# A new order of the same instructions on every engine of a two-layer decoder kernel

## Chip, cores and metric

The kernel runs on one core of one Trainium2 chip. A core has TensorE (PE in the profile, with its weight loads as PEld), VectorE (DVE), ScalarE (ACT), GpSimd (POOL) and SyncE (SP, which here only issues DMAs). The metric is the device time of one execution in microseconds (us), the median of the runs. Everything is in 32-bit floats.

## What is computed

Eight sequences of 256 rows by 256 columns go through six blocks, each added to its input and followed by a layer norm:

```python
x = _layernorm(x + _L0_attn_ref(...))   # selective scan: in-projection, convolution of 4 taps, 16 states, gate, out-projection
x = _layernorm(x + _L0_xattn_ref(...))  # cross term with the context, 192 columns
x = _layernorm(x + _L0_ffn_ref(...))    # feed-forward, 1024 hidden, low-rank experts, best two of four
x = _layernorm(x + _L1_attn_ref(...))   # attention, 16 query heads, 4 key heads, rotary
x = _layernorm(x + _L1_xattn_ref(...))  # cross attention to the context
x = _layernorm(x + _L1_ffn_ref(...))    # recurrent gates, carried from sequence to sequence
```

The state of the last block runs through the eight sequences in order, and all outputs need the final state. So the program ends with a short stage for all eight sequences at once.

## The kernel before

One sequence is a batch b, from 0 to 7. The work on it is cut into streams, one letter each. F is the front of the scan block (norm, projections, convolution, softplus, gates). S is the scan itself: 16 steps of [128 x 1024] for each batch. G is the gate, out-projection and norm behind the scan. W holds the cross term and the feed-forward of batch b (the x functions), between them the last two blocks of batch b-1 (the z functions), and at the end the final stage (the e functions). Y is the attention's projections and scores, V its values and out-projection. Every stream is a Python generator on each engine; a piece between two `yield`s is a unit.

Nothing sorts the work at run time. Each engine takes its instructions strictly in program order. That order is written out by hand or by a planner in the table `ORDER`: a string of letters for each engine, and `play` lets the stream named by each letter go on by one unit. Inside a stream the order is fixed. Between the engines semaphores hold everything in place, so that any order without a deadlock computes the same.

The streams overlap. While DVE scans batch b, PE works on the attention of b-1, on the feed-forward of b-1 and on the front of b+1. One scan step on DVE is three instructions in SBUF alone: the product for the next step (line 567), the scan (576), the product with C (584). From the third batch on, a DMA that GpSimd issues (609) adds halves of the result before PE turns and sums it (512).

The norms tie GpSimd to DVE. `stats_end` takes mean and variance on DVE; its last instruction (267) writes the variance. GpSimd then runs `rstd`: a power (275) and a product (276), both of [128 x 2]. ScalarE applies them (`normal`, 279), and PE turns the result (`turn`, 286). Each batch has seven such places: a (front), a1 (behind the scan), b1 and f1 (W, first half), c2 and c1 (W, second half) and t (V). An eighth one, rn, has two powers (881) behind DVE's 805. Over eight batches that makes 64 places. The t place has one more power behind it (1375).

Lines that the prediction speaks of, beside these: 1311 and 1312 are the rotary products (one input in PSUM), 1336 is the maximum of the scores (input in PSUM), 1349 the weighing of values, 1342 a reciprocal of [128 x 4], 1103 and 1104 the update of the recurrent state (two inputs in SBUF), 1201, 1210, 1229 and 1234 the matmuls of scores, turns, row sums and values.

```python
def rstd(pool, own, tag):
    own.link(pool.tensor_tensor(ln_rs[tag][:, :], ln_var[tag][:, :], neghalf[:, 0:T], ALU.pow))
    return pool.tensor_tensor(ln_nb[tag][:, :], ln_nm[tag][:, :], ln_rs[tag][:, :], ALU.mult)
```

Of the kernel before, what the change touches and what calls it, by code (L numbers as in the profile page):

```python
# [44 lines left out]

ORDER = {
    "pe": (
        "FFFFFFFFFSSWFSFFSWSYSWSYFSFSFSFYSWSSSSSSFYGGGFGSSYYWWWYYWYWYSFYSWYWYWSYWWWFYWYFSSWWWWFWSWWSWWWWWSSYYYYYYYSYYSY"
        "SYYYYYSWSYYVSYFYVYGGGYYGYVSSYWWYWVYWYFSWYFYVYWSWFWYVYWWWSYWYWVWYWWFWYYSVWWSVWWSWWWVFVVSYSWWYYWYWYSWFYWYYYSYWSY"
        "WWYWWYSWWSYWWYSYVYSFYGYVYGWGGYYSSYWWVWYSYVWYWYFYFYWVWYWSYSVWYWYWSWYVWYWFWYWSYVWVSWWVWWWWWSVVFSYWFYWYYWSYWYYWYY"  # L50
        "WYSWYSWWYWWSYWYWWYSYSWYVFSYYGGYVWFYGYVYGFYYSSYWWWYSFWVWYSFYSWWWVYYFWYWWYVYWWSYWVWWYYWVSWWVWWWWWSVSVVWFSYWYYSWY"
# [9 lines left out]
        "YSWYWSSYWSYYSSWWSWFSSWYYSYWYYSYSVWYYYGYSSWVGYYYYSFGSSWYYVWYYSVSFYYFYYWWYVYFWYSYSSWVWYYWSYYWSVSYWYFWYYSVSWFSWFS"
        "WSWWSFYWFVWSWSYWSWYYSWYWSSYWSWSYSYSWYWYYYWSSWSYYVYYFSGSYYFVGSYYWVFYYYYGSSWYFWFSYYSVYFFSSWSWFYYWYVYWWYYWSYYWVSS"
        "YWYVWYYWVSWFWSSSWWSSWYFSWVWWYSWWSWSYYYSSWSWYYSWYWSSYYWYYSWSYVSYYYFSSWSYGGVYYYYGYVSWSYYWFYYSYYVFSFYWYSWFSYVWYFW"
        "FWFSWYYWYYFSVWWYYVSSWYYWWFSSVSSSWWWSYVWWWSWSYSYWSWYSSWYSYWYSWYWFSSYYWYYSWSYVYSYSYSFWVSGYYGYYYYGVSWYYFWSVYYFYYS"
        "FWVWYYSYWYSFSWFYVYWWYYSSVFWYYWYYWVWWSSWSSSWWFSYSSVWSYYSWWWSYWFSSWYWYYYSWWSYYSYWYWSSYYWVSFSSYYSWGVYYGSYYSWFYVGY"
# [5 lines left out]
        "FWFFFFFSWSFSSSFSFSSSSSFSSSSSSWSYFFSFSSSSSSSSFSFYSWSSFSWSSSSWSSSSWSSSSSSSFSSYGGSSGSSGSSYSSYYFWYYSYWYSFYYWSSWWFY"
        "SSYSFSSSWSSWSYFSSSWWYSSSSSWWSSSSYYSSSYSSSYSSYSSYYSSSYFSYYSGVYGSSYYSSVGYSYGYFSFYVSSYYWSSVYWYFSVYSWYSWWSYVYFWSYF"
        "SWFSYSVWYSYSSWSVSSSWSSWWSVVSSSYSYSSWSFSWYSYSWSSYSSSSWSSYYSSWYSFYVYGGYSSSYYSVGGSSYYYSFYVSFSWSVYYWYSSYSYWVSWYWFY"
        "YSYWVSSSYWYSWSVYFSVSFWSSSSWFSWWSVVSSYSYFSSSSYWSYWSWSSYSSSSSWYYSYSSWYYSYVGGSFSYYSYVFFGSYYVSGYSSYSSSYWFSWFFVYYYF"
        "WSWWSYSYVYWSYSVYWSYSSVYSWSWVSSSSSWWWVSSSVSYSSFYSWSSYWSWYSSSSYWSSSYSYSSYWYYSVSGGYYYSSSYVSGGYYSSYVFSSSFWYYFWYYSY"
        "SVSFWYVWWFYYFFSWSWYSSVYYWSYVSSWSSSSSFSVWWWSSVVSSSYSSYSWSSWYSWSYSSYSSSWSYYSSYWSYYFSVYSSGGYVYSSGYGYYSFFSYVSYYSWV"
        "SYWYSYVFWSWYWSYYFVFYWSWYYSVSYSSWVSSFWSSVSSSSWWWSSVSYSYSSSSYSSSYWFSWYSWSSYYSSSSWYYYSSWSSFSVSYGGYYSSSYGVGYYSSVSY"
        "SSYYWSVYWSYYSVWYSWWSYYSVYWSSWYYSSYWVSSSWVSFSWSSWWVSSSVSSYSSYSWSWYSWSYSSYSWSSYYSSSSYYYWGGYYVYYGGYYVYVWYYWVYYYWV"
        "YWWVYYYWYYYWVWWVWVWWVYYYYYYYYWYYVWWYYYVYYYVYYWYVYYYWVYWYVYYYVYYVVVWWWWWWWWWWWW"
# [1697 lines left out]
```

## Time and profile before

| | us |
|---|---|
| median of 3 runs | 1268.45 |
| lowest, highest | 1267.79, 1273.7 |
| the profiled execution, its own time | 1271.64 |
| its span in the profile | 1268.9 |
| PE busy in the span | 1103.8 (87%) |
| DVE busy | 1025.4 (81%) |
| ACT busy | 762.8 (60%) |
| POOL busy | 219.6 (17%) |

The profile is one execution. Its span lies 2.74 us below its own device time, and that time lies 3.2 us above the median. In a timeline row the first number is the start from the span's begin, the second the duration, both in us. A bracket behind a row tells how long the engine sat idle before it and who released it. Ends of neighbouring instructions on DVE overlap by some 0.08 us in the records, and matmuls overlap more, so sums of single durations exceed the busy time.

### The profile page before, as it was taken

The numbers are of one execution on the slowest core, as the hardware profiler recorded it, in microseconds if no ns is written. First come the engines' busy times: TensorE is split into PE (matmuls) and PEld (weight loads), VectorE is DVE, ScalarE is ACT, GpSimd is POOL, SyncE is SP. The second block draws the span as 40 slices with busy tenths as digits, with TensorE's granted clock in tenths as the row PEclk, the third lists the DMA queues.
The fourth block names the chain that finished last, engine by engine and source line by source line (L and its number), as shares of the span: only waits on it lengthen the run. The fifth ranks groups of instructions, "written<-read, shape, count | busy, mean of one in ns | idle before, by whom it ended". The sixth has DMA issues, their size and how long they took to land.

```text
span 1268.9 us, 17417 instructions
## 1 busy us (share of the span) xinstructions
PE 1103.8 (87%) x6154; PEld 805.9 (64%) x6154; DVE 1025.4 (81%) x1690; ACT 762.8 (60%) x2010; POOL 219.6 (17%) x257
## 2 busy tenths in 40 slices
...
DMA packets 41193, 86.70 MB, mean 68 GB/s; under 512 B 3737, under 2 KB 14970, under 8 KB 40466
## 3 DMA queue, kind: packets, MB, share of 16 engines
...
q8 instruction: 48, 0.79, 0.3%
...
## 4 chain that ended last, share of the span: by engine, by line
PE 45%; DVE 28%; ACT 12%; issue 6%; POOL 5%; DMA 4%; ACTq 0%; DVEq 0%; SPq 0%; POOLq 0%
PE bank L292 14%; DVE scans L576 7%; DVE scans L584 4%; PE bank L1201 4%; PE bank L927 3%; DMA scans<-scans 3%; PE bank L1234 3%; PE bank L921 3%; PE bank L512 3%; PE bank L1210 3%; DVE conv L431 2%; ACT scans L541 2%; PE bank L692 2%; DVE scans L567 2%; PE bank L1143 2%
## 5 line engine op out<-in xcount | busy, mean ns | idle before, releaser
L541 ACT ACTIVATE scans<-dt,a_neg 128x255 f32<-128x255 f32 x512 | 225.2, 500 | 0.1
L609 POOL DMA_DIRECT2D scans<-scans x96 | 84.6, 881 | 512.6 <-DVE scans L584 512.4
L576 DVE TENSOR_TENSOR_SCAN scans<-scans 128x1024 f32<-128x1024 f32 x64 | 146.2, 2285 | 13.5 <-ACT scans L541 12.8
L584 DVE TENSOR_TENSOR scans<-scans,BC 128x1024 f32<-128x1024 f32 x128 | 155.9, 1218 | 0.1
L576 DVE TENSOR_TENSOR_SCAN scans<-scans,dBx_odd 128x1024 f32<-128x1024 f32 x64 | 146.2, 2285 | 9.2 <-ACT scans L541 9.2
L512 PE MATMUL bank<-ident,scans 128*128 128x128 f32 x640 | 105.3, 303 | 45.0 <-DVE scans L584 29.4
L1282 ACT ACTIVATE ya<-bank,nmax 128x256 f32<-128x256 f32 x256 | 117.9, 474 | 41.8 <-issue 23.5
L512 PEld LDWEIGHTS bank<-ident,scans 128*128 128x128 f32 x640 | 83.8, 156 | 70.0 <-DVE scans L584 35.2
L1336 DVE TENSOR_REDUCE nmax<-bank 128x2 f32<-128x512 f32 x128 | 83.6, 683 | 38.4 <-PE bank L1201 38.1
L1289 ACT ACTIVATE ya<-bank 128x512 f32<-128x512 f32 x128 | 73.3, 602 | 27.5 <-PE bank L1210 26.7
L1210 PE MATMUL bank<-ident,ya 128*128 128x128 f32 x512 | 76.1, 280 | 8.4 <-ACT ya L1282 8.4
L538 ACT ACTIVATE scans<-neghalf 128x4 f32<-128x4 f32 x128 | 26.6, 208 | 88.4 <-PE bank L512 88.3
L567 DVE TENSOR_TENSOR scans<-conv,BC 128x1024 f32<-128x1024 f32 x64 | 77.5, 1211 | 0.1
L567 DVE TENSOR_TENSOR dBx_odd<-conv,BC 128x1024 f32<-128x1024 f32 x64 | 77.4, 1209 | 0.0
L1201 PE MATMUL bank<-kT,qT 64*128 64x256 f32 x512 | 72.6, 402 | 5.1 <-ACT ya L1289 4.2
L1210 PEld LDWEIGHTS bank<-ident,ya 128*128 128x128 f32 x512 | 59.6, 143 | 27.4 <-ACT ya L1282 17.5
L1234 PE MATMUL bank<-ya,v 128*64 128x256 f32 x512 | 67.7, 386 | 2.4 <-ACT ya L1289 1.7
L692 PE MATMUL bank<-w_i,xT 128*128 128x512 f32 x128 | 67.2, 651 | 1.4 <-ACT wa L783 1.4
L292 PE MATMUL bank<-w_q,yT 128*128 128x512 f32 x128 | 61.6, 604 | 0.0
L1201 PEld LDWEIGHTS bank<-kT,qT 64*128 64x128 f32 x512 | 44.1, 186 | 27.3 <-issue 16.9
L1245 PE MATMUL bank<-w_ao,qT 128*128 128x256 f32 x256 | 60.3, 386 | 0.0
L737 PE MATMUL bank<-w_o,wa 128*128 128x256 f32 x256 | 57.4, 380 | 0.0
...
## 6 DMA issues: line engine op xcount, KB each, us to landing
...
```

Source lines behind the costliest of these rows:

```text
L292: last = pe.matmul(o, l, r, start=(start and i == 0), stop=(i == n - 1), skip_group_check=True)
L512: last = pe.matmul(sums_of(c, t), step_of(b, u)[:, i, t * P:(t + 1) * P], ident[:, :], is_transpose=True, start=False, stop=(h == UH - 1 a ...
L541: ins = act.activation(step[:, j, 1:S], dt[b % 2][:, c, 1:S], ACT.Exp, scale=a_neg[:, c, n:n + 1])
L567: dve.tensor_tensor(dBx[u % 2], conv[b % 2][:, c:c + 1, :].to_broadcast([P, HN, S]), Bh, ALU.mult).then_inc(s["a_dBx"], 1)
L576: dve.tensor_tensor_scan(H, H, flat(dBx[u % 2]), 0.0, ALU.mult, ALU.add).then_inc(s["a_scan"], 1)
L584: dve.tensor_tensor(H, H, Ch, ALU.mult).then_inc(s["a_hC"], 1)
L609: pool.dma_start(flat(H[:, 0:2, :]), flat(H[:, 2:4, :]), accum_op=ALU.add).then_inc(SUM_OF[(NU * b + u) % 3], 16)
L692: pe.matmul(WB[j % 2][:, :], xT[:, k, t * P:(t + 1) * P], w_i[:, k, half * 512:(half + 1) * 512], start=(k == 0), stop=False, skip_group_c ...
L1201: last = pe.matmul(YB[i][:, t * S:(t + 1) * S], qT[half, p, t * P:(t + 1) * P], k[half], start=True, stop=True, tile_position=(half.start, 0))
L1210: last = pe.transpose(YB[h % 2][:, k * S + t * P:k * S + (t + 1) * P], pe_[:, h % 2, t, k * P:(k + 1) * P], ident[:, :])
L1234: last = pe.matmul(y2[i * HD:(i + 1) * HD, 0:S], v1[:, k, g, :], pT[:, i, k, :], start=(k == 0), stop=(k == 1), tile_position=(0, i * HD))
L1282: act.activation(pe_[:, h % 2, t, :], YB[h % 2][:, t * S:(t + 1) * S], ACT.Exp, bias=nmax[:, h % 4, t:t + 1], accum_out=ls[:, p % 2, t, h ...
```

## The change

No instruction, tile, wait or DMA is added or removed; each stream keeps its own order. Only the strings in `ORDER` are new, for all five engines, with the same count of each letter. Counted out against the units, GpSimd's and SyncE's orders move by at most 6 places. On PE the units before the last G unit are 825 before and 820 after: one score unit, two turns, one value unit and one turn of W now stand behind it. On DVE they are 864 and 860.

What stands on DVE directly behind the instruction that releases GpSimd (line 267 or 805), by place and batch:

| place, batch | before | after |
|---|---|---|
| a, 1 | 584, 576 | 1470, 584 |
| rn, 1 | 584, 576 | 431, 431 |
| c2, 0 | 576, 1356 | 452, 1356 |
| c1, 0, 1 and 4 | 584, 576 | 1311, 1312 |
| a1, 2 | 584, 576 | 1336, 1336 |
| b1, 2 | 1342, 584 | 1349, 1342 |
| c2, 2 | 1356, 259, 576 | 1356, 259, 264 |
| a, 7 | 584, 1342 | 1336, 805 |
| c1, 5 | 567, 1311 | 1311, 1312 |
| a, 5 | 597, 259, 567 | 576, 1336 |
| rn, 4 | 1336, 1336 | 576, 1336 |
| a1, 6 | 1336, 1336 | 584, 1103 |

Over all 64 places the next instruction is one with both inputs in SBUF (443, 447, 567, 576, 584, 814, 1103, 1104) or a large copy-like one (1080) 21 times before and 8 times after.

```diff
     "pe": (
...
-        "WWSVSVVWYSWYYWYWYSWYYWYSWYYWWYSWYYSWYWWYYWSYWVYYSSYGGWGGVYYYWWWYVYWYWVYYYVWYWYWVWYWWYYWWYVWYYWWVWVWWVWWWWWVVYW"
-        "YYYYYYYYYWYWYYWYWYYVWYWYYWYWVWYYWYVWYYWYVWYYWYVYYVYWYYVYWYYVVVVVWWWWWWWWWWWWWWWWWWWWW"
+        "WSWVVVYVSWVWYSYYWYYWSYWYYWYWYYWYSWYWWWWWYYSSSYGWGGGYVYWYWWWVYYWYWVYYYVWYYWYVWYYWVYWYWYWWYVWYYWWVWVWWVWWWWWVVYW"
+        "YYYYYYYYWYYWYYWYWYYVWYWYYWYWVWYYWYVWYYWYVWYYWYVYYYVYWYVYWYYVVVVVWWWWWWWWWWWWWWWWWWWWW"
...
     "pool": (
-        "FFFGWWWSGFSWSWSSSSSSWWVSSSWSSSSSGSFWSWSSSSSSWWSVSSWSSSSSFSGSWSWSSSSWSWSVSSWSSSSSGSWSFWSSSSSWWSVSSSWSSSSSGFSWSW"
-        "SSSSSWWSVSSSWSSSSSGSSWWSSSSSSWWVSSSWSSSSGWWWWVWWVWWWWWW"
+        "FFGWWFWFSGWSWSSSSSSSSWWVSSSSWSSSGSFWWSSSSSSWWSVSSSSWSSSSSGSFWSWSSSSSSWWVSSSSWSSSGSSSFWWSSSSSSWWVSSSWSSSSGSSFWS"
+        "WSSSSSSWWSVSSWSSSSGSSWSWSSSSSSWWSVSSSWSSGWWWWVWWVWWWWWW"
     ),
     "sp": (
-        "WFFSWSSWFWFSGWSSFSSSWFGSSWFFSWGWSSWSFSFWWWGWSSSFWSWWGSWFSSFSFWWWGWSSSFWSWGWWSSSGWWWWWWWWW"
+        "WFSFWSSWFWWSGSSWFFSSGFSSSFSGWWWFWSSSFSGWWWFSWSSFSGWWFWSSWFSSWFGWWWSSFSSWGWWSSSWWGWWWWWWWWW"
     ),
```

## Rows read from the trace of the kernel before

**Rows 1.** The page, part 1: busy time, share of the span, instructions; and part 4, engines.
```profile
PE 1103.8 (87%) x6154; PEld 805.9 (64%) x6154; DVE 1025.4 (81%) x1690; ACT 762.8 (60%) x2010; POOL 219.6 (17%) x257
...
PE 45%; DVE 28%; ACT 12%; issue 6%; POOL 5%; DMA 4%; ACTq 0%; DVEq 0%; SPq 0%; POOLq 0%
```

**Rows 2.** Busy time by stretch: the stretch, its length, each engine's busy time, granted clock, DMA.
```profile
0.00:200.00 200.00, 136.59 (x545) 91.51 (x546) 170.21 (x224) 94.97 (x220) 14.17 (x22) 0.79 0.28 99
200.00:1070.00 870.00, 795.38 (x4613) 590.63 (x4612) 776.88 (x1229) 571.67 (x1535) 187.13 (x198) 0.96 0.30 69
1070.00:1200.00 130.00, 123.61 (x785) 88.11 (x784) 52.52 (x153) 72.03 (x206) 8.21 (x17) 1.00 0.10 35
1200.00:1269.00 69.00, 48.22 (x217) 35.69 (x215) 25.76 (x86) 24.17 (x53) 10.14 (x20) 0.92 0.09 31
```

**Rows 3.** GpSimd's four small lines: duration ns min/median/max, then each line's busy total.
```profile
L275 POOL TENSOR_TENSOR rstd_c<-var_c,neghalf x16: 688/1593/2785, 323.3 to 1229.7; 128x2 f32<-128x2 f32 x16
L276 POOL TENSOR_TENSOR shift_c<-minus_c,rstd_c x16: 194/196/2115, 326.0 to 1230.5; 128x2 f32<-128x2 f32 x16
L881 POOL TENSOR_TENSOR rn<-ss,neghalf x16: 679/699/2135, 150.6 to 1083.0; 128x2 f32<-128x2 f32 x16
L1375 POOL TENSOR_TENSOR rstd_c<-var_c,neghalf x8: 683/689/1717, 329.1 to 1213.6; 128x2 f32<-128x2 f32 x8
...
sum 1269.00, POOL 63.28; mean POOL 63.28
...
sum 1269.00, POOL 40.39; mean POOL 40.39
...
sum 1269.00, POOL 15.62; mean POOL 15.62
...
sum 1269.00, POOL 8.48; mean POOL 8.48
```

**Rows 4.** Timeline of DVE and GpSimd at place c1 of batch 1.
```profile
495.32 1.22 DVE L584 TENSOR_TENSOR scans<-scans,BC 128x1024 f32<-128x1024 f32 x1
496.46 2.29 DVE L576 TENSOR_TENSOR_SCAN scans<-scans,dBx_odd 128x1024 f32<-128x1024 f32 x1
...
495.50 1.61 POOL L275 TENSOR_TENSOR rstd_c<-var_c,neghalf 128x2 f32<-128x2 f32 x1 [9.54 <-DVE var_c L267]
497.19 1.54 POOL L276 TENSOR_TENSOR shift_c<-minus_c,rstd_c 128x2 f32<-128x2 f32 x1
```

**Rows 5.** Timeline of DVE and GpSimd at place a of batch 3.
```profile
264.55 2.28 DVE L576 TENSOR_TENSOR_SCAN scans<-scans 128x1024 f32<-128x1024 f32 x1
...
264.32 0.69 POOL L275 TENSOR_TENSOR rstd_a<-var_a,neghalf 128x2 f32<-128x2 f32 x1 [2.54 <-DVE var_a L267]
265.09 1.73 POOL L276 TENSOR_TENSOR shift_a<-minus_a,rstd_a 128x2 f32<-128x2 f32 x1
```

**Rows 6.** Timeline of DVE and GpSimd at place c1 of batch 2.
```profile
636.58 0.69 DVE L1311 TENSOR_TENSOR ya<-bank,rope 128x512 f32<-128x512 f32 x1
...
636.76 0.71 POOL L275 TENSOR_TENSOR rstd_c<-var_c,neghalf 128x2 f32<-128x2 f32 x1 [4.70 <-DVE var_c L267]
637.55 0.19 POOL L276 TENSOR_TENSOR shift_c<-minus_c,rstd_c 128x2 f32<-128x2 f32 x1
```

**Rows 7.** Chain of waits, POOL's first and last lengthened places: start, length, what.
```profile
42.88 1.61 POOL rstd_a L275
...
44.56 1.57 POOL shift_a L276
...
1039.90 1.62 POOL rstd_c L275
```

**Rows 8.** Waits, 200 to 1070 us, DVE and PE: total us, times, longest.
```profile
DVE scans L576 <- ACT scans L541: 19.8, 12, 4.8
...
PE bank L286 <- ACT x L279: 10.3, 7, 1.9
PE bank L286 <- ACT xb L279: 6.7, 3, 3.2
```

**Rows 9.** What line 1311 waited for in the whole span: us, times.
```profile
  PE bank L292: 25.0, 11
```

**Rows 10.** Chain of waits behind 1160 us, PE's attention units.
```profile
1162.93 1.06 PE bank L1201 x8
1163.99 0.58 PE bank L286 x4
1164.58 0.59 PE bank L1229 x8
1165.16 0.86 PE bank L1234 x8
...
1167.95 0.87 PE bank L1210 x8
```

More of the change, by code:

```diff
@@ L47 @@
     "pe": (
[L48 to L51, printed above, removed]
@@ L52 @@
-        "WYWSYWYWYYSWYYWYWWSYWYWWYSYWYVSFYYSYWGVGYGYGYVSSYYWWWFYWVWSYYYFSFWYYVWWFYSWVWWFWWYYWYWWVSWFYYWWVWWSWWSVWSVVVWF"
-        "YWYSWYWSYWYYSYWYWYSWYWYYWWYWYSWSWYYWYVSYFYSWVYGGGYYGYVSSYWYWWYVWFYSWYYFVWWYSWYFYWVWYWYWSVYWWYWYWVWSVWWVWSWWWSW"
-        "VFVYSFWYYYSYWYYWYSWYWYSFYWSYWYWYWWWSYYWYWWYSVSYWFSYGVGGYYGWYVSSWYYWWVSYWYWYVYWSYWWYSVYWWWYYWSWYWVWWYYSWVWWVWWW"
-        "WWSVSVVWYSWYYWYWYSWYYWYSWYYWWYSWYYSWYWWYYWSYWVYYSSYGGWGGVYYYWWWYVYWYWVYYYVWYWYWVWYWWYYWWYVWYYWWVWVWWVWWWWWVVYW"
-        "YYYYYYYYYWYWYYWYWYYVWYWYYWYWVWYYWYVWYYWYVWYYWYVYYVYWYYVYWYYVVVVVWWWWWWWWWWWWWWWWWWWWW"
+        "FFFFFFFSFSFWWSSSWFYYYFSFSSSSSFFSSWYFSSSSGGGFGSSYSWWWWYYSWSYWYWWYYSWFWWWFWSWSWYWWYSFWWSYWWWWYFSFWYFSYYYYYYYYSSY"
@@ new lines @@
+        "YYFYSYWYSYYYVSGFYGGYGYVSYYWSWWFYWWVFYYYSVWWWYYYSVWYYSYFWVWFWYWSYWYWSWVWYFSWWYWVWWWWVSVVVWSYSFWYWYWSYYWYWYYSYYW"
+        "SYWYYWSYWWYYWWSYWSVGYWYGGGYVSYWYWSYWVWYSYWYWFVYYFYWVWYWYSFYWVWWYSYWSWYWFWWVWSYWWWYFWWWWSVVVSVVYWFYSWYWYWSYWYWY"
+        "SYWYYSWYWSYWYWYWWYSWYYFSSYWGVYGGYGVYSYSWYWVSYYWWYWSYWFYVFYVYWYSWYFVWWYYWYWSVWWYFYWFVSWWVWSWWVWVWWWWSSVFYWYWYSW"
+        "YWSYYYWYYWWYSYYSWWSYWYWWSYYWYSWWVGYGYGGYWSVSFYYWSWWYVWYYYVWYSYSYFVWYYWYWFSWVWYYWFSWWYVWYYSWWVWFWWFVWWSWWWSVVVY"
+        "FWYSWYWYWSYWYYYWYSYWYSYWWYWYSWWWYSWSYWGYVGGGYWSYSVYWFYWYWYSWVWYSFYYVWFWYSYWYVSYYWYWWFWWYVYWSYVFYWFWYSWVVWWSWWW"
@@ L57 @@
+        "VSWWVSVFYWYWYYWYSWYWYYSYWYWYSYWWYWYWSWWSWSWGYGGGYSFSWYWWWVYYWSYWVSYYVWYWWSYYVWYWSYWYWWYVWYSYWWYVWYYSWWYWWWVYYS"
+        "WSWVVVYVSWVWYSYYWYYWSYWYYWYWYYWYSWYWWWWWYYSSSYGWGGGYVYWYWWWVYYWYWVYYYVWYYWYVWYYWVYWYWYWWYVWYYWWVWVWWVWWWWWVVYW"
+        "YYYYYYYYWYYWYYWYWYYVWYWYYWYWVWYYWYVWYYWYVWYYWYVYYYVYWYVYWYYVVVVVWWWWWWWWWWWWWWWWWWWWW"
     ),
     "act": (
-        "FFFFFFFFFSSFFSSFSSSSFFSFSSSSFFSSFSFSSFSFSSFSSSSSSSWSSSSFSSGSFSGSSGFWSWSFSWWSSWFSWFSWSWFFWSWSWSWSWSSSSWSWSYYSSS"
-        "SYYSYSYSFYYSYYYSSYSSYYVSYYWVSGFYYGYYYVGYWYYWFSVSYYFSYYSFYWVWYSYWSYVFFWYWYWFYYWWSWVSYYFWYYSSSWVSSWSWWFWYSSWSVWW"
@@ L61 @@
[L61 to L65, printed above, removed]
@@ L66 @@
-        "WYSYSWVYYYSYSVWYWYYWSYSSVWYWYWYYSWSWYYVWYSSYWVWWSSSWSWWSYSVWWSWWSSYYWYWSYSWWSYSWYYSSYYWYYWYWYYVYGWGYYYYVGWYYWY"
-        "YVYYYVYWYWYYVWYVWWYYWYYWYYWVYYWVWWWWWYWYYVYWYWYWYYWYYYYWVWYYYYWWYYYWYVYYYYVYWYWVYYWYYYVYVWYYYYWVYYWYYVVWWWWWWW"
+        "FFFFFFFFFSSSFSFSSSFSSSSSSSFFFSSSSFFSSSSSSSSFFFSSSSSSSSFSSSSGWFGGWSSWSSSSWWWSFSWFWSSWWSFWSSWWFWSFSSWFSFSFWYSSSY"
+        "SYFSYYYSYSYFSSYYYSYWSYFGYSSGYVYSFYYVGYWSYSWFYYVYYWFWVSYYWYYFSFYYSVSYWYWFYSWYSWSSVYWYFWYVWSSFYYWYSWSVSWSWWSSYSV"
+        "WWSWSWFSYWYWYSSYSYSWYYWYYWSYSYSSWYYGSVYWGWYSYYGYYWWVSSYYWYVYFSYFYVSYYWWYFYYWYVSFSWFYWVYWFYYSWWSSSWVYFWYWSWSFYY"
@@ new lines @@
+        "VSSWSWYSWSVWWSWYWSYSWYWYSSSSWWSYYSWYFYWYSSYYYSYSGWFVYYWGSSYYYVGYSSWYVYYWYSWSYFYFYYSSVFYWYVWYYSWYYFSWYVFYWWYFYV"
+        "SWYFYSWFWVSWSWSSWSSWWYFWVSSWWWYSSSYWSYWWSYYSWYSWSSYYSYWSYYWSYWSWYGGSYVYWYGYVSSYWSYFWSVYYYYYYYYVSSFYWYWYYSVFWYS"
+        "FWYWSSWYVYFSWFVYYWYFYWSSWFWSFWSVSWSYWSWVSWWWSWYSYSWYYWYSSSYWWSYFWSYSYWSSYWYWGSGYYSYVWYSGVSYYYWYFWSYYFYVSYFSSWV"
+        "WYYWYYFYYSYYWSVWYSWFYWVYYFSFSSYWFYVYWYFWVSWSSWSSSSWWYWSWVFWWYSYWSWYYWSSSWYWSYYWSSWYSSWWGSGYYSYGSWSWYYWYVYSYFYY"
+        "VSYSWSWVYWYYYVSWSWYYSYWYWSVYYWYYWSSYVYWYYWSSYYVWSYSYVSWWSYWVSWSWSWYSWSYYWWYSYYWYWSSWYYWYYWGYYGWYYGWVWYYWYYVYYY"
@@ L68 @@
+        "YVWYYWYYVWYVYYYWVWYYWYYWYVYWYYWVWWWWWYVYYWYYYWWWYYWYYYYWWYYYYVWWYYYVYWYYWYYVYYWYVYWYYVYYYWYVYYWYYVYYVVWWWWWWWW"
         "WWWWWWWWWWWWW"
@@ L70 @@
     "dve": (
[L71 to L79, printed above, removed]
+        "FFFFFWFWSSSSSSFSSFSFWSSSSSSSSWYSSSFSSSSSFWSSSSSFSSWSFSSYSSSFSSSSSSSSSFSYSGGSSSSGSGWYSSSYSSWSSSWYSYFYSSWYFWYWSY"
@@ new lines @@
+        "SSSSWWSSFSSSYWSWFYSFFSSYWSSWYYSSSSYFYSSSYSYSFSYSSSYYSYFSFYSGGYSSGSYVGYYSSYVSSSYYWFWYVSSYYSSWVYFWYYWYFSVFSYSSYS"
+        "WSYSWSVSYSYWSVSFWYSSSSSWSWVWFVSVSSSSSYYSSWSYSWSYFSWYSSSYYSWSSYSSYYGSGSYSSGVGYYWSYFVYYSSSYWSVYYWVYSSYSYWFWYWVSY"
+        "YFVWYFSSFWSYYSSWSWSYSSVSWFSWWVSSSVVSSSSYSSYSWSWYSSWYSSSYSSSYSYWSYSFSYSYGGSSVYSSGYYGWFSVYYYSSVYFSYSWYSSYWYVYSSF"
+        "YWVYWYWSSYFVYYWFFSYVSSWSSFWSSVWSSSSVWSSWWVSSSYSSYSSSSYWSYSWSWYSSSSYSYSFSSYSYWGYGSWSYSGGYYVSSVYSSSFYSYVFYWSYYSW"
+        "YVYSYSYSWYYWWVSFYSWVSSWYYFFVYSFSWSSWSSSSWFSVWWVSVSSSYSSSYSWSYSWSYSWYSSSSYSSYSSYSGWGSWYSYGGSYVFSYYSVYSSFFYWYSSW"
@@ L80 @@
+        "YYVYSSSWSWVYYYWSFYYVYSWSSFVFYSFYYWSYSSVSWSWVSSSSWVSSWWSVSFYSSSYSSSYWSSYWFWYSSSSWSSYSSSGGYSSYGGSWSYYSSSYSWVSYYW"
+        "VYFSSYYWSVWYWSYYSSYVWSSYYWSSVYSYWYSSWYSVYYSSWVSSYSWWVSSSVVSSYYSSSSYWSSYWWYSSSYSYSWGYYYGWGYGYYVVWYYYWYVYYYVWYYW"
+        "WYVYYVYWYYYVWWWVVWWWVYYYYYYYWYYYWWVYYYVYYYYVYYVWYYYYWVWYYYVYYYVVVVWWWWWWWWWWWW"
     ),
     "pool": (
-        "FFFGWWWSGFSWSWSSSSSSWWVSSSWSSSSSGSFWSWSSSSSSWWSVSSWSSSSSFSGSWSWSSSSWSWSVSSWSSSSSGSWSFWSSSSSWWSVSSSWSSSSSGFSWSW"
-        "SSSSSWWSVSSSWSSSSSGSSWWSSSSSSWWVSSSWSSSSGWWWWVWWVWWWWWW"
+        "FFGWWFWFSGWSWSSSSSSSSWWVSSSSWSSSGSFWWSSSSSSWWSVSSSSWSSSSSGSFWSWSSSSSSWWVSSSSWSSSGSSSFWWSSSSSSWWVSSSWSSSSGSSFWS"
```

1 line of the change is left out of this document (added).

## The prediction

> **What bounds the kernel now.** Read first the busy shares and the chain's engines on the page, then the busy time by stretch, then GpSimd's lines, then timelines around them. PE is busy for 87% of the span and DVE for 81%; the chain that ended last runs 45% through PE, 28% through DVE, and 5% through POOL, which is 63 us of it for an engine that is busy only 17% [rows 1]. By stretch there are four regimes [rows 2]. Up to 200 us DVE leads (170.2 of 200 us) and PE starves. From 200 to 1070 us both are nearly full: PE 795.4 of 870 us, idle for 74.6; DVE 776.9, idle for 93.1. From 1070 to 1200 us PE alone bounds (123.6 of 130 us, DVE 52.5). The last 69 us are a short serial end. No engine in the long stretch has another that it could simply wait for: what is lost there is lost in small waits where one in-order engine stands for another. PE's work is the same before and after, so time can come only out of PE's idle time.
>
> The edit is aimed at one source of such waits. A power of [128 x 2] on GpSimd takes 0.69 us at the least and the product behind it 0.19, but single ones take 2.8 and 2.1 us [rows 3]. The timeline tells why. At c1 of batch 1, DVE starts line 584 (two inputs in SBUF) just before GpSimd starts the power; DVE ends at 496.54 and GpSimd at 497.11. The product then starts inside the scan and ends with it, at 498.73 against 498.75 [rows 4]. At c1 of batch 2 DVE runs 1311 in the same place, one input of which is in PSUM, and power and product take 0.71 and 0.19 us [rows 6]. So a GpSimd instruction that begins inside a DVE instruction with two SBUF inputs waits for that one's end (a power ends some 0.56 us behind it, a product with it). Sum it up: the four lines are busy for 63.28 + 40.39 + 15.62 + 8.48 = 127.8 us, and at their smallest durations they would be 56 x 0.688 + 56 x 0.194 + 16 x 0.679 + 8 x 0.683 = 65.7 us [rows 3]. 62 us are waiting inside GpSimd. I followed the chain of waits piece by piece and set each GpSimd piece against its smallest duration: 19 places on it before 1070 us are lengthened, by 36.8 us in all; the first is a of batch 1 (1.61 and 1.57 us, so 2.3 too much), the last c1 of batch 5 (0.9 too much) [rows 7].
>
> **Part 1: what the new order takes from the locks.** For each of the 64 places I read which DVE instructions follow the releasing one in the new order and applied the rule above, with DVE's own durations (about 2.29 us for a scan, 1.22 for 584 or 567). A two-input instruction stands directly behind in 8 places in place of 21. Of the 19 places on the chain, 11 become free: rn 1, c2 0, c1 0, a1 2, c1 1, c2 2, a 7, b1 5, c1 4, b1 6 and c1 5; together they cost 21.9 us. The other 8 fall from 14.9 to 7.0 us, as only the product or a later piece is still caught. That is 29.8 us off. Against it, new waits come where there were less: a 5 (+2.2), rn 4 (+2.1), a 6 (+1.6), a1 6 (+1.6), a1 5, rn 3 and t 2 (+1.0 each), and four smaller ones (+2.1), 12.6 in all. The same share of them as now, 36.8 of 62, should lie on the chain: 7.4 us. Net 22 us less on the chain. Over all places the same count gives 69 us before, where 62 are measured, and 38 after; so I expect some 34 us of lock time in the new profile.
>
> **Part 2: how much of it arrives.** A step of the chain that gets shorter by 2 us only helps until the next-latest input sets the start. The ends are 0 (another input is always as late) and the whole 22 us. Rows that speak for much: PE stood still 17 us in ten waits before turns of norms that GpSimd feeds [rows 8]. For little: GpSimd's delay is only one of many causes, DVE waited 19.8 us in the same stretch for the exponentials of ScalarE [rows 8], and all four engines are in order. 17 us of PE's waits in that stretch against 36.8 on the chain is a little under one half, so I take one half: 11 us, with 0 and 22 kept as ends.
>
> **Part 3: what moves between the head and the tail.** Behind the last G unit PE now has one score unit, two turns, one value unit and one turn of W more. By the chain's rows these take 1.06, 2 x 0.44 (half of the row of eight each), 0.59 + 0.86, and 0.58 us [rows 10]: 4 us more for a stretch that PE bounds. The head is shorter by these 4 us where PE sets the pace, and by 1.9 us where DVE does (two maxima, a reciprocal and a weighing fewer before the last G unit). I take between none and 2 us lost, and use 1.5.
>
> **Part 4: edits at no cost.** GpSimd's own queue and SyncE's move by at most 6 places; 96 DMA issues on GpSimd stay in the same order to each other, and DVE's next scans cover them. Should a fold's DMA come later than now, PE's sum waits. Every order must also put waits somewhere: the work that DVE now does in front of a scan is mostly work that reads PSUM, so DVE waits for PE there if PE is late; line 1311 already does so 11 times for 25.0 us [rows 9]. What is queued behind it is the scan, for which PE, GpSimd and ScalarE wait in turn. I have no row of the new order that shows it. It can be nothing, or 2.3 us for each of the 13 places where a one-input instruction comes first now (30 us). I take nothing, as in c1 of batch 2, where 1311 already stood first, it started at once [rows 6].
>
> **A rule that would speak against it.** GpSimd's power at a 3 ran from 264.32 to 265.01 and DVE's scan started in the middle of it, at 264.55, and took 2.28 us like any other [rows 5]; DVE doesn't wait for GpSimd. The Trainium skill (SBUF — State Buffer, section on SBUF's two separate sides) has the shared ports as an exclusive lock: whoever starts first, DVE with two SBUF inputs or GpSimd reading SBUF, keeps the other out for its whole instruction. Its one half is what the rows show; by the other half each place where GpSimd begins just before a two-input DVE instruction would cost DVE up to the rest of a power, and the new order has more of these (10 against 6 by the count of the second instruction): some 2 us more. I leave that out of the sum.
>
> **Sum.** 11 us arrive, 1.5 are lost: 9.5 us off. Against the profiled execution, 1271.6 - 9.5 = 1262.1; it lies 3.2 us above the median of the runs, so 1258.9 us, 0.75% below 1268.45.
>
> **Rivals.**
> - The next-latest input steps in. For it: both PE and DVE are over 89% full in the long stretch [rows 2], and much of the chain is PE following itself. Against it: a lock of 2 us stands on ScalarE's and PE's way together. At a quarter or less of 22 us arriving, less 1.5: 4 us, 1264.5.
> - DVE is held in front of its scans. The place is behind lines 267 and 805, where now PSUM readers stand before 584 or 576. Price: 25.0 / 11 = 2.3 us for each place in which PE is late [rows 9]; it ends slower by more than 0.5% from 7 late places of 13 on (7 x 2.3 = 16.1 against the 9.5 gained, 6.6 us too much). With 8: 18.4 - 9.5 = 8.9, 1277.
> - The whole net 22 us arrive, as in-order engines pass every delay on: 22 - 1.5 = 20.5, 1248.
> - The order doesn't do what it says: on the chip the engines meet elsewhere than the order puts them, a GpSimd piece is caught by other instructions, and the lock time stays at some 60 us. For it: DVE's waits shift what runs when. Against it: my count from the order alone gave 69 for a measured 62. Time 1268, with the 1.5 us of the tail 1270.
>
> **How the numbers follow.** Chances: the forecast 0.45, the next-latest input 0.24, DVE held 0.16, the whole gain 0.10, no effect 0.05. About 0.5% (6.3 us) is what a measurement can tell from no change. Of the forecast 0.40 lies below 1262.1 and 0.05 above; the next-latest input gives 0.04 faster and 0.20 same; DVE held 0.15 slower and 0.01 same; the whole gain 0.10 faster; no effect 0.02 same and 0.03 slower. Together faster 0.54, same 0.28, slower 0.18. The range goes from 1243 (the whole gain, with some of its own spread) to 1278 (DVE held as priced); most of the likeliest case's own range is 1253 to 1264.
>
> **What the changed profile would show.** Right: busy time of lines 275, 276, 881 and 1375 near 100 us in place of 127.8; the chain's share of POOL near 3%; PE idle between 200 and 1070 us down from 75 us by some 10; fewer and shorter waits before line 286. The tail from the last G unit on longer by some 2 to 4 us. Rival one: the lock time falls but PE's idle time doesn't. Rival two: DVE's waits for PE at 1311, 1336 and 431 grow beyond the time gained. Wrong altogether: lock time near 60 us. The forecast is wrong above all if the order as a whole, and not its places behind 267 and 805, decides; one order differs from another in hundreds of neighbourhoods that I haven't priced.

## The result, and the profile after

| | before | after |
|---|---|---|
| median, us | 1268.35 | 1205.72 |
| lowest, highest | 1267.79, 1273.7 | 1203.47, 1209.99 |
| ratio, 95% interval | | 0.9501, 0.9462 to 0.954 |
| the profiled execution, its span | 1271.64, 1268.9 | 1203.95, 1202.2 |

The new order takes 62.6 us (5%) off. The forecast was 9.5 us; the time lies 37 us below the range. In the tables below microseconds against before are a run's ratio less 1, times 1268.4; runs that are compared with each other were, with the exceptions named, set against the same runs of before. One execution each of two kernels of the experiments was disturbed (3714 us with the scan units moved back, 5331 us in the new order with neither locks nor folds) and is left out, with its trace.

The page of after, parts 1 and 4 (the lines that answer [rows 1]), and the busy time by stretch (for [rows 2]; the long stretch ends 70 us earlier here):

```profile
PE 1076.3 (90%) x6154; PEld 796.0 (66%) x6154; DVE 1021.4 (85%) x1690; ACT 761.0 (63%) x2010; POOL 197.5 (16%) x257
...
PE 56%; DVE 28%; ACT 7%; issue 6%; POOL 2%; DMA 1%; ACTq 0%; DVEq 0%; SPq 0%; POOLq 0%
...
0.00:200.00 200.00, 137.13 (x534) 95.93 (x535) 168.97 (x221) 91.31 (x216) 12.70 (x22) 0.75 0.27 95
200.00:1000.00 800.00, 763.71 (x4589) 573.28 (x4588) 772.18 (x1229) 570.70 (x1530) 166.39 (x198) 1.00 0.33 76
1000.00:1130.00 130.00, 123.98 (x799) 88.81 (x799) 53.05 (x154) 73.20 (x208) 8.23 (x17) 1.00 0.09 31
1130.00:1202.00 72.00, 51.52 (x239) 38.03 (x238) 27.15 (x88) 25.76 (x57) 10.15 (x20) 0.91 0.13 45
```

The stretch in which DVE and PE are both nearly full had 870 us [rows 2] and has 800. In it DVE is now idle for 28 us where it was for 93, and PE for 36 where it was for 75. PE's granted clock there is 1.00, after 0.96 [rows 2]. Over the span, PE's idle time fell by 39 us, from 165.1 to 125.9, and its busy time by 27.5, from 1103.8 to 1076.3, with the same 6154 matmuls. PE was busy at half clock for 116.9 us before and for 73.1 after; half of the difference, 22 of the 27.5 us, is the clock, an estimate (a matmul of line 692 takes 590 ns at full clock and 1201 at half).

GpSimd's lines (for [rows 3]: first the start and duration of one group, then the busy totals of lines 275, 276, 881 and 1375):

```profile
L275 POOL TENSOR_TENSOR rstd_a<-var_a,neghalf x16: 690/712/2748, 5.5 to 1002.9; 128x2 f32<-128x2 f32 x16
...
sum 1202.00, POOL 49.07; mean POOL 49.07
...
sum 1202.00, POOL 25.70; mean POOL 25.70
...
sum 1202.00, POOL 18.66; mean POOL 18.66
...
sum 1202.00, POOL 11.45; mean POOL 11.45
```

Together 104.9 us, 39 over their smallest durations; it was 127.8 and 62. The last start of the first group, which is a1 of batch 7, the norm behind the last scan, is at 1002.9, where it was at 1073.4: 70.5 us of gain up to there, and some 4 us are given back in the tail. On the chain of waits, POOL's pieces fell from 62.9 to 24.0 us, and what they had over their smallest durations from 36.8 to 11.9.

Waits from 200 to 1000 us in after, DVE's first lines and then PE's (total us, times, longest; for [rows 8]):

```profile
DVE zg L591 <- PE bank L512: 5.1, 1, 5.1
DVE nmax L1336 <- PE bank L1201: 3.0, 6, 1.6
...
DVE scans L576 <- ACT scans L541: 2.0, 5, 0.8
...
PE bank L1201 <- ACT ya L1289: 8.1, 9, 1.3
PE bank L512 <- DMA scans<-scans: 4.2, 3, 2.6
...
PE bank L286 <- ACT xb L279: 2.2, 2, 1.9
```

The two waits before the turns at 286 that [rows 8] shows went from 17 us to 2.2. But two others went as well, and neither has a norm in it: DVE's scans waited 19.8 us for ScalarE's exponentials [rows 8] and wait 2.0, and PE waited 15.6 us for the folding DMAs and waits 4.2. The row of before for the latter:

```profile
PE bank L512 <- DMA scans<-scans: 15.6, 8, 5.0
```

### The profile page after: what moved, and what is told of

It reads as the page before. It is cut to its first block, busy times and chain, and to the rows that moved or that the text cites. A ratio compares the mean times of both kernels' runs of the same rounds, so it can differ in the third digit from the quotient of the medians.

```text
span 1202.2 us, 17418 instructions
## 1 busy us (share of the span) xinstructions
PE 1076.3 (90%) x6154; PEld 796.0 (66%) x6154; DVE 1021.4 (85%) x1690; ACT 761.0 (63%) x2010; POOL 197.5 (16%) x257
## 4 chain that ended last, share of the span: by engine, by line
PE 56%; DVE 28%; ACT 7%; issue 6%; POOL 2%; DMA 1%; ACTq 0%; DVEq 0%; SPq 0%; POOLq 0%
PE bank L292 17%; DVE scans L576 8%; DVE scans L584 4%; PE bank L1245 4%; PE bank L1201 4%; PE bank L737 4%; PE bank L927 3%; PE bank L921 3%; PE bank L512 3%; PE bank L1143 3%; PE bank L1234 2%; PE bank L1210 2%; PE bank L692 2%; DVE conv L431 2%; DVE nmax L1336 2%
## 5 line engine op out<-in xcount | busy, mean ns | idle before, releaser
L576 DVE TENSOR_TENSOR_SCAN scans<-scans 128x1024 f32<-128x1024 f32 x64 | 146.2, 2284 | 0.8 <-ACT scans L538 0.6
L512 PE MATMUL bank<-ident,scans 128*128 128x128 f32 x640 | 103.1, 300 | 28.9 <-DVE scans L584 24.6
L692 PE MATMUL bank<-w_i,xT 128*128 128x512 f32 x128 | 63.8, 622 | 0.7 <-ACT wa L783 0.7
```

Source lines behind the costliest of these rows:

```text
L512: last = pe.matmul(sums_of(c, t), step_of(b, u)[:, i, t * P:(t + 1) * P], ident[:, :], is_transpose=True, start=False, stop=(h == UH - 1 a ...
L576: dve.tensor_tensor_scan(H, H, flat(dBx[u % 2]), 0.0, ALU.mult, ALU.add).then_inc(s["a_scan"], 1)
```

## Experiments

The theory as it stood behind the result: in-order engines pass every delay on in full, so the 23 us of lock time less, with what PE's clock adds, carry most of the gain (theory A). Rivals: the order as a whole carries it (theory B), by way of the folding DMAs (theory C) or of the work that stands ready (theory D); or the clock does (theory E).

**1. The locks out of both orders.** GpSimd's 136 small instructions become memsets, which read nothing; they took some 38 us in all in both kernels. This leaves the norms' factors out of the computation. It also takes off work: without locks the originals would be 65.7 us.

```diff
-    own.link(pool.tensor_tensor(ln_rs[tag][:, :], ln_var[tag][:, :], neghalf[:, 0:T], ALU.pow))
-    return pool.tensor_tensor(ln_nb[tag][:, :], ln_nm[tag][:, :], ln_rs[tag][:, :], ALU.mult)
+    for _ in range(4):
+        own.link(pool.memset(ln_rs[tag][:, :], 0.5))
+    return pool.memset(ln_nb[tag][:, :], 0.0)
```

> Order of before; GpSimd's powers and products (lines 275, 276, 881, 1375) are replaced by memsets of the same tiles, four linked ones for a power and one for a product. They read nothing, so I expect that VectorE's two-input instructions do not hold them: about 0.65 and 0.1 us each, busy total of these lines near 50 us in place of 127.8. The norms are left out by this. Theory A (the locks, passed on several times over by an order that was tight without them): most of the 62.6 us comes back, 1205 to 1220 us. Theory B (the new order as a whole is better, the locks are a small part): 1245 to 1258 us.

> The same replacement in the order of after, where 39 us of lock time are left. Theory A: these are where the order has room for them, so a small gain, 1195 to 1205 us, and about the same time as the order of before without locks. Theory B: 1198 to 1205 us too, but some 45 us below the order of before without locks. The norms are left out by this.

Measured: 1237.28 us in the old order (ratio 0.975, 0.9715 to 0.9785) and 1199.18 in the new one (0.9454, 0.9424 to 0.9484). The first lies between the two theories, the second where both had it. With no lock in either, the orders still differ by 37.5 us (by the intervals, some 6 either way). So some 37 of the 62.6 us don't come from GpSimd's waiting.

**2. The direct places changed by DVE's order alone.** A place is called direct here when a two-input instruction stands right behind line 267 or 805. Three kernels move units in DVE's string only. The first puts 17 scan units of the new order back directly behind 267 or 805 (25 direct places in place of 8); the second moves PSUM readers of the old order up in 48 steps, so that 2 places are direct in place of 21; the third does that at 7 places of the new order (2 direct in place of 8). One line of each of the last two (old order, new order):

```diff
-        "SWFSYSVWYSYSSWSVSSSWSSWWSVVSSSYSYSSWSFSWYSYSWSSYSSSSWSSYYSSWYSFYVYGGYSSSYYSVGGSSYYYSFYVSFSWSVYYWYSSYSYWVSWYWFY"
+        "SWFSYSVWYSYSSWSVSSSWSSWVVWYSSSSSYSSWSFSWYSYSWYSSSSSSWSSYYSSWYSFYVYGGYSSSYYSVGGYYYSSSFYVSFWVYSSYWYYSSSYWVSWYWFY"
...
-        "WSYSWSVSYSYWSVSFWYSSSSSWSWVWFVSVSSSSSYYSSWSYSWSYFSWYSSSYYSWSSYSSYYGSGSYSSGVGYYWSYFVYYSSSYWSVYYWVYSSYSYWFWYWVSY"
+        "WSYSWSVSYSYWSVSFWYSSSSSWSWVWFVSVSSSSSYYSSWSYSWSYFSWYSSSYYSWSSYSSYYGSGSYSSGVGYYWSYFVYYSSSYWVYSYWVYSSYSYWFWYWVSY"
```

> Order of after; in VectorE's string alone, at 17 of the 19 places that had a two-input instruction directly behind line 267 or 805 before and no longer have it, the next scan unit is moved up to stand there again (by 1 to 3 units). Direct places go from 8 to 25. Theory A: locks of about 1 to 2 us at 17 places, most of the loss is back, 1235 to 1268 us. Theory B: up to 1215 us.

> Order of before; in VectorE's string alone, behind line 267 or 805 units that read PSUM or are small are moved up in front of the scan units (at most 5 units away), 48 moves, direct places go from 21 to 2. Theory A: lock time falls from 62 to some 30 us and with it much of the 62.6 us, 1215 to 1240 us. Theory B: 1255 to 1275 us, as moving PSUM readers up makes VectorE wait for TensorE.

> Order of after; in VectorE's string alone, at 7 places that still have a two-input instruction behind line 267 or 805, nine units that read PSUM are moved up (at most 3 units away). This could beat both kernels. Theory A: of the 6.5 us that locks still cost, 2 to 4 come back, 1201 to 1204 us. Theory B (as in the old order with 48 such moves, VectorE waits for TensorE instead): 1206 to 1220 us.

Measured: 1223.24 us (18 slower than after, ratio 0.963, 0.96 to 0.966; under theory A's 1235 and over theory B's 1215), 1316.57 (48 slower than before, ratio 1.0364, 1.0335 to 1.0392, beyond both theories), and 1213.59 (8 slower than after by the medians, 5 by the ratio, 0.954, 0.951 to 0.9571, as theory B had it). The second is the telling one. It did what it says: GpSimd's four lines fell to 45.28 + 16.53 + 10.87 + 7.50 = 80.2 us, less than in after. Its waits behind 200 us, DVE and PE:

```profile
DVE nmax L1336 <- PE bank L1201: 45.0, 27, 3.5
DVE x L1356 <- PE bank L1245: 16.1, 6, 3.4
DVE yo L1311 <- PE bank L292: 15.6, 2, 11.5
...
PE bank L512 <- DMA scans<-scans: 37.0, 20, 5.4
```

DVE stands before PSUM readers that come too early, the scans behind them start late, and PE waits for their sums. PE was also at half clock for longer: 102 us between 200 and 1100 us, where before had 68. Fewer locks bought with DVE's order alone cost more than they save, in either order: 9.3 us of lock time less in the third kernel came with some 5 to 8 us more, though in that one the intervals touch.

**3. The folding DMAs out.** From the third batch on nothing is folded (line 609 gone) and half of the states are left out of the result; alone, and together with the memsets of 1, in both orders.

```diff
-                pool.dma_start(flat(H[:, 0:2, :]), flat(H[:, 2:4, :]), accum_op=ALU.add).then_inc(SUM_OF[(NU * b + u) % 3], 16)
```

> Order of before. From the third batch on GpSimd waits for the product as before but issues no DMA that folds the halves, and TensorE waits for VectorE's product (line 584) itself; it still sums two of the four slices, so its work is unchanged, and half of the states is left out of the sum. Theory C (beside the locks, the old order lies too tight behind the folding DMAs: TensorE waited 15.6 us for them, and the chain without locks runs 74 us through them): 1235 to 1255 us. Theory D (TensorE's waits for the DMAs are as harmless as they are short, and the rest is in the order itself): 1260 to 1270 us.

> Order of before, without folding DMAs and with GpSimd's powers and products as memsets (norms and half of the states left out). Theory C: both causes gone, 1195 to 1212 us, near the new order without locks (1199.2). Theory D: 1228 to 1238 us, as without locks alone (1237.3).

> Order of after without the folding DMAs (half of the states left out). TensorE waited for them 4.2 us there. Theory C and D: 1198 to 1206 us; a larger gain would say that the new order is not free of them either.

> Order of after without folding DMAs and without locks (norms and half of the states left out). The floor of this order: 1192 to 1199 us. Set against the same version of the order of before it gives what the new order has beyond both causes: under 10 us by theory C, 35 us by theory D.

| ratio to before (95%) | old order | new order |
|---|---|---|
| as it is | 1 | 0.9501 (0.9462 to 0.954) |
| no locks | 0.975 (0.9715 to 0.9785) | 0.9454 (0.9424 to 0.9484) |
| no folds | 0.994 (0.9919 to 0.9961) | 0.9481 (0.9459 to 0.9502) |
| neither | 0.9563 (0.9544 to 0.9581) | 0.9439 (0.9418 to 0.9459) |

(First two lines and last two lines are two sets of runs.) The third line is where theory D had it (1262.1 us), the old order without both lies 2 us above theory C's 1212 (1214.06 us), and the two of the new order are as expected. In the old order each hides the other: the folds cost 7.6 us beside the locks and 24 us without them. In the new order neither is worth more than 6 us alone, and both together are worth 8. With both gone the orders differ by 16 us (some 3 either way). Laid one behind the other, locks first, the 63 us of the ratio are 26 that end with the locks, 22 more that end with the folds, and these 16. For them the traces show where the old order still waits more; DVE from 200 to 1020 us, first in the old order without both, then in the new one without locks (that without both has no trace):

```profile
DVE nmax L1335 <- PE bank L1200: 10.5, 14, 2.6
DVE scans L574 <- ACT scans L539: 9.7, 5, 3.5
...
DVE nmax L1339 <- PE bank L1204: 5.5, 7, 2.8
...
DVE scans L577 <- ACT scans L542: 1.3, 4, 0.4
```

**4. Why the folds are late.** Around PE's longest standstill in the long stretch of before; the timeline of GpSimd and SyncE, and then three windows (length; busy time of PE, PEld, DVE, ACT, POOL; granted clock; DMA share; GB/s):

```profile
553.10 0.37 SPq L483 DMA_DIRECT2D BC<-xpj_scratch  x1
553.43 0.90 POOL L609 DMA_DIRECT2D scans<-scans  x1 [2.88 <-DVE scans L584]
...
555.00:556.00 1.00, 0.34 (x4) 0.00 (x0) 0.97 (x3) 1.00 (x4) 0.00 (x0) 1.00 1.04 291
...
555.40:557.60 2.20, 0.00 (x0) 0.00 (x0) 2.10 (x9) 2.13 (x6) 0.79 (x2) 1.00 1.00 241
557.80:567.80 10.00, 6.74 (x20) 4.45 (x20) 7.04 (x17) 5.07 (x16) 0.00 (x0) 0.50 0.15 33
```

The same end of a line 584 lets SyncE issue a 1 MB load of B and C (483) and GpSimd the fold; the load goes first, all 16 DMA engines are full at 240 to 290 GB/s, PE stands still for 5.0 us (555.3 to 560.3), and from 557.7 on its clock is 0.50 for 10 us. It isn't a single case. Of the 96 folds of before, 23 were issued within 6 us behind or 2 us ahead of such a load; they landed a median 5.8 us after the end of their issue, the other 73 after 2.4. In after it is 24 at 5.9 and 72 at 2.4. The new order doesn't avoid the meeting. Three kernels load one state of four from the third batch on (256 KB; the rest is multiplied by old values), the middle one with the memsets of 1:

```diff
+                n = HN if b < 2 else 1
-                sp.dma_start(BC[:, h % 2, :, :], scratch[b % 2][0:2 * NS, :].rearrange("(i n) s -> i n s", i=2)[:, h * HN:(h + 1) * HN, :]
+                sp.dma_start(BC[:, h % 2, :, 0:n * S], scratch[b % 2][0:2 * NS, :].rearrange("(i n) s -> i n s", i=2)[:, h * HN:h * HN + n, :]
```

> The order of before; from the third batch on, the broadcast loads of B and C that SyncE issues (line 483) bring one state of four, 256 KB in place of 1 MB, with the same issues and waits; VectorE multiplies by the old values for the rest. The folding DMAs stay. In the trace of before 19 of the 96 folding DMAs landed over 4 us after their issue's end, and 18 of them were issued within 6 us behind such a load (median 5.8 us to landing against 2.4 for the others); TensorE's longest standstill (5.0 us at 555.3) ends with one. Theory M (the fold is late because it meets the load): landings over 4 us fall from 19 to under 5, TensorE's waits for folds fall from 15.6 us to under 5, and the time is 4 to 12 us lower, 1256 to 1264, as much as leaving out the folds gave (6.3 us or more). Theory N (the fold's own 2.4 us and the longer chain behind it are what costs): landings get shorter, the time stays within 2 us of before.

> As the run before, and GpSimd's powers and products are memsets (no lock). The kernel without locks took 1237 us, and without locks and folds 1214. Theory M: most of these 23 us are the meeting of fold and load: 1214 to 1224. Theory N: it is the folds themselves, in whatever time they land: 1232 to 1238.

> The new order with the loads cut to 256 KB from the third batch on. The folding DMAs met the loads there as often (24 of 96, median 5.9 us to landing), but TensorE waited only 4.2 us for them, and leaving out the folds gave 1.8 us. Theory M: within 3 us of after, 1203 to 1206, though the landings get shorter as much as in the old order; the new order doesn't avoid the meetings, it has other work ready. Against it: more than 5 us lower would mean that the loads slow more than the folds do.

Measured: 0.9959 (0.9939 to 0.9979), 5 us less; 0.9642 (0.96 to 0.9685) beside the locks' removal, 14 us less than the memsets alone (by the intervals, some 7 either way); and 0.9455 (0.9431 to 0.9478), 1201.51 us, 4 to 6 less than after, a little more than foreseen. The small loads weren't short enough to clear the way: folds near one still landed after 4.6 us, and 17 of 96 over 4 us, where 19 did before and theory M wanted under 5. PE's row of the first kernel, for the 15.6 us above (line numbers one up), and then that of the memsets alone and of the second kernel:

```profile
PE bank L513 <- DMA scans<-scans: 8.7, 6, 3.6
...
PE bank L513 <- DMA scans<-scans: 19.8, 10, 5.2
...
PE bank L514 <- DMA scans<-scans: 12.0, 9, 3.8
```

So theory M's times were met in the old order and its mechanism only in part: about half of what the folds cost the old order without locks (14 of 24 us, both rough) goes when the load is smaller. That all of it goes through the folds isn't shown: in the new order the small loads brought 4 to 6 us, more than the 3 foreseen, and leaving out the folds only 2.5. In the new order the meeting is as frequent, and PE waits 4.2 us for folds.

**5. The price of a late GpSimd.** Linked memsets before each of the 56 powers: six in the new order, six in the old one, three in the new one.

```diff
+            for _ in range(6):
+                own.link(pool.memset(ln_rs[tag][:, :], 0.5))
             own.link(pool.tensor_tensor(ln_rs[tag][:, :], ln_var[tag][:, :], neghalf[:, 0:T], ALU.pow))
```

> Order of after; six linked memsets in front of each of the 56 powers of line 275, some 1.1 us more on GpSimd each time, 60 us in all, about as much as the locks add in the order of before. Theory A, if the price of such lateness is the same in both orders (31.6 us per 62 us): 1230 to 1240 us. Theory C (the new order has room for lateness of GpSimd wherever it comes): 1208 to 1220 us.

> The order of before with the same six linked memsets of [128 x 2] ahead of each of the 56 powers of line 275, some 1.1 us each time by the run on the new order, 60 us in all. The question is whether the old order pays the same price for a late GpSimd. Lateness is passed on in full in either order (1.15 us per us there): +69 us, about 1337 us. The old order was already late in places, so that the next-latest inputs cover part of the delay: +35 to +55 us, 1305 to 1325. The old order is the more sensitive one (its delays also send PE down to 1.2 GHz, 68 us of it already): +80 us or more, 1350.

> The new order with three linked memsets ahead of each power in place of six, about half the delay: some 0.55 us each time, 31 us in all. If the new order passes lateness on in full from the first half microsecond on: +31 to +37 us over after, 1237 to 1243 us. If it has room for a little and none for more: under +15 us, below 1221, while six memsets cost 69. Clock part: with small delays PE's standstills stay short; fewer than ten dips of the granted clock below 2.4 GHz between 200 us and the last gate.

Measured: 1274.71 us (1.0026, 1.0008 to 1.0044), 1322.7 (1.0395, 1.0365 to 1.0425) and 1234.07 (0.9703, 0.9679 to 0.9728). Six memsets delay a power by 0.97 us in the middle case and three by 0.50; from the first memset to the power it sums to 55.7, 56.5 and 28.9 us. A delay also changes which instructions are caught. At c2 of batch 1 power and product took 0.69 and 0.66 us in after (443.95); half a microsecond later the scan had started (timeline of the third kernel, DVE and GpSimd, lines two up):

```profile
460.60 0.41 POOL L276 MEMSET rstd_c<- 128x2 f32 x3
460.92 2.29 DVE L578 TENSOR_TENSOR_SCAN scans<-scans,dBx_odd 128x1024 f32<-128x1024 f32 x1 [0.32 <-ACT scans L543]
461.08 2.61 POOL L277 TENSOR_TENSOR rstd_c<-var_c,neghalf 128x2 f32<-128x2 f32 x1
463.77 0.61 POOL L278 TENSOR_TENSOR shift_c<-minus_c,rstd_c 128x2 f32<-128x2 f32 x1
```

The first is slower than either theory had it (1240 at most), the second in its middle case (1305 to 1325), the third between its two (1221 and 1237). The cost has to be laid against all of GpSimd's time at these places: the four lines' busy time and the inserted delay.

| GpSimd's time, us | old order | new order |
|---|---|---|
| 38 (no locks) | -31.7 | -69.3 |
| 104.9 (after) | | -63.3 |
| 127.8 (before) | 0 | |
| 157.7 (128.8 + 28.9) | | -37.7 |
| 180.7 (124.2 + 56.5) | +50.1 | |
| 184.3 (128.6 + 55.7) | | +3.3 |

(us against before.) Each microsecond of GpSimd costs the old order 0.35 up to 127.8 and 0.95 behind it; the new one 0.09, then 0.48, then 1.5. The first of these, 6 us in 67, isn't clear of the runs' own spread (some 6 us); the others are. The expectations took one price for an order; here it rises with GpSimd's time. Between the points the new order is 52 us faster at GpSimd's 127.8 us, and by the same reckoning 52 at 180.7. What is left of the 63, 11 us, is the fewer locks at the new order's own price, 22.9 x 0.48. At the old order's price, 0.35, they would be 8.

**6. The clock.** Into the new order, ten places of the same sum (batches 2 to 6) get PE work that adds zeros: 24 matmuls back to back, or 10 that each wait for the last. The inserted time is 55.3 and some 53 us (twice what was meant: one matmul in 32 bits is two passes of 275 ns at the median).

```diff
+                for n in range(10):
+                    last = pe.matmul(sums_of(c, n % 2), nought[:, 0:1].to_broadcast([P, P]), ident[:, :], start=False, stop=False,
+                                     skip_group_check=True)
+                    last.then_inc(s["filler"], 1)
+                    pe.wait_ge(s["filler"], 10 * k + n + 1)
```

> Order of after; at ten places (in front of scan sums 5 and 11 of batches 2 to 6) TensorE gets 24 more matmuls of [128 x 128] against a column of zeros, back to back, about 2.6 us each place, 26 us of busy work in all that changes no value. TensorE's clock should stay up. Theory E (a wait of TensorE lowers its clock and so costs more than its own length) and theory F (a wait costs its length): 1215 to 1235 us, half-speed time between 200 and 1100 us under 20 us.

> The same ten places, but ten such matmuls each of which waits for the one before, so that TensorE mostly stands still for about 2.5 us at each place. Theory E: half-speed time behind most of the ten places (30 us or more), and 8 to 20 us slower than the busy version. Theory F: within 5 us of the busy version for the same inserted time.

Measured: 1258.11 us (0.989, 0.9859 to 0.9922), so 52 us more than after for 55.3 inserted, and 1263.79 (0.9936, 0.9911 to 0.996). The second kernel's PE, in the inserted places alone:

```profile
  PE bank L496: 22.4, 90
```

With 22.4 us of standing still in place of work, in 90 pieces of a quarter of a microsecond, the median is 5.7 us longer though some 2 us less were inserted. That is between theory F (within 5) and theory E (8 to 20), and the intervals of the two overlap. In the profiled executions, 1267.94 us with the idle filler and 1254.85 with the busy one, PE was at half clock for 24 us of the long stretch against 3.4, and its busy time was 6 us longer though it had 280 passes less. But the four pieces at half clock (421, 820, 868 and 960 us) don't stand behind the inserted places: the nearest begins 16 us behind the end of one, and from 440 to 450 us, around the place at 442, the clock is 1.00. So the short standstills of the filler are not shown to lower the clock, and theory E's "behind most of the ten places" failed.

The executions of one kernel differ in the clock too, and this gives its price without an insertion. Those of the idle filler go from 1260.07 us at a mean granted clock of 0.953 to 1267.94 at 0.945; 0.008 less is some 20 us more at half clock (2 x 0.008 x 1264), for 7.9 us. Those of after give 6.5 us for 17 (1203.47 at 0.952, 1209.99 at 0.945), those of the new order with six memsets 5.1 for 18 (1271.76 at 0.94, 1276.89 at 0.933). That is 0.3 to 0.4 us for each microsecond at half clock; which of the two brings about the other these rows can't tell. Over the span before has 165 us at half clock and after 115, so at this price 15 to 20 of the 62.6 us go with the clock, an estimate; they are part of what the locks, the folds and the rest bring, not a sum beside it. In 200 to 1090 us before was at half clock for 68 us in 14 pieces, after for 3.4 in one.

**7. SyncE's old order with the rest of the new one.**

```diff
-        "WFSFWSSWFWWSGSSWFFSSGFSSSFSGWWWFWSSSFSGWWWFSWSSFSGWWFWSSWFSSWFGWWWSSFSSWGWWSSSWWGWWWWWWWWW"
+        "WFFSWSSWFWFSGWSSFSSSWFGSSWFFSWGWSSWSFSFWWWGWSSSFWSWWGSWFSSFSFWWWGWSSSFWSWGWWSSSGWWWWWWWWW"
```

> The new order on TensorE, VectorE, ScalarE and GpSimd, with SyncE's string of before: the loads that SyncE issues come in the old order. This is the one engine whose old string can be put beside the new strings of the others without a deadlock. If SyncE's order carries part of the 15 us that neither GpSimd's waiting nor the folding DMAs account for: +4 to +15 us over after, 1210 to 1221 us, with more waits of TensorE for DMAs. If the gain lies in the orders of TensorE and VectorE together: within 2 us of after, 1204 to 1208.

Measured: 1225.15 us (0.9632, 0.9598 to 0.9666), 17 us slower than after by the ratios (some 7 either way), 19 by the medians. Both theories had it faster, and neither had the place right: PE's waits for DMAs stay (6.2 us), and DVE, which had none behind 200 us in before or after, now waits for loads:

```profile
DVE ln_st_f L259 <- DMA xin<-in_x: 7.6, 1, 7.6
DVE conv L597 <- DMA conv<-in_x: 5.8, 3, 3.3
```

In the old order the same string of SyncE causes no such waits, so it isn't what made the old one slow. It shows that the new strings fit each other: with SyncE's, whose units move by at most 6 places, left behind, 17 of the 62.6 us are lost. The converse, SyncE's new string in the old order, wasn't run.

## Why the prediction was wrong

*What bounds the kernel.* Right as far as it went: two nearly full engines, losses in small waits. It read PE's 1103.8 us as fixed ("time can come only out of PE's idle time"). That was wrong by 27.5 us of busy time, 22 of them the clock. The row that says so stood there: a granted clock of 0.96 in a stretch where after has 1.00 [rows 2]. 68 us of it were at half clock, in 14 pieces that each begin in a standstill of 1.0 to 5.0 us or within 3 us behind it, as in the windows of experiment 4; ten other standstills of 1.0 to 2.0 us had no such piece. How much of the busy time is time of the kernel is less certain; experiment 6 puts 8 us on 20 us at half clock.

*Part 1, the locks.* Right: some 34 us of lock time forecast, 39 measured; four lines near 100, 104.9 measured; on the chain 22 us less forecast, 25 measured (36.8 to 11.9). DVE's scans are again not longer for a GpSimd instruction that began before them (2284 ns the median, 2294 and 2297 the longest of the two kinds of scan, against 2293 before), so leaving the second half of the rule out of the sum was right. The Trainium skill (SBUF — State Buffer, section on SBUF's two separate sides) has the port lock as exclusive for either side; in these runs only GpSimd is kept out. One piece doesn't fit "begins inside": the power at 834.17 in after began 0.22 us ahead of a scan and still ended 0.48 us behind it, after 2.99 us.

*Part 2, how much arrives.* As a price, one half is near the new order's own between 104.9 and 157.7 us: 0.48 us for each, 11 us for 22.9, the very figure of the forecast. With prices from 0.09 to 1.5 in the same order, the match is in part luck. What failed is the step behind it, that this product is the gain. The price belongs to the order and to how late it already is, and by the old order's own, 0.35, the same locks are worth 8 us. Depending on the reckoning, the locks carry from 8 to 25 us (62.6 less the 37.5 without them) of the gain.

*Part 3, the tail.* Right: about 4 us given back in a tail that PE bounds, but the head gained 70 us, so it hardly mattered.

*Part 4, "edits at no cost".* This is the step that was wrong. It looked at what the other moves could cost and found nothing; what they could bring it left out, and said that hundreds of neighbourhoods hadn't been priced. They bring 37 to 55 us. It looked at GpSimd's and SyncE's moves, of at most 6 places, and at DVE's behind 267 and 805; counted the same way, units move by up to 39 places on PE, 43 on ScalarE and 46 on DVE. What of this has been shown: 24 us is the folds' cost in the old order without locks against under 2 in the new one, about half of it gone with a smaller load; the waits for ScalarE's exponentials went from 19.8 to 2.0 us, and the memsets alone bring them only to 11.3. The folds' row wasn't among those I had chosen, because no norm was in it; but the chain's engines stood in [rows 1], with DMA at 4% (1% in after) and ACT at 12% (7%) beside POOL's 5%. Some 16 us remain between the two orders with neither locks nor folds (1214.1 and 1198.5). These I can't assign: in the first PE was at half clock for 24 us, and DVE waited longer for the exponentials and the scores (experiment 3), but single strings can't be exchanged without a deadlock, except SyncE's, and two at once weren't tried. It stays open.

*The rivals.* "DVE held by PSUM readers" didn't happen in the change, where DVE's waits for PE in the long stretch fell from 48 to 16 us, but experiment 2 shows it is real: 48 us slower from moves in DVE's string alone. It would have been the forecast for a change of that kind. "The whole gain" had the right sign of the miss, its ceiling of 22 us didn't. Every case in the list drew on one cause, and so did the range; that is why it ended at 1243.
